# Retention stage: the output projection as three one-pass products on split operands, the decay sums as two

## The reference, cut to what matters

```python
qkvg = x @ w_attn                                  # x normalised; 16 q heads, 8 k and v heads of 64, 8 gates
log_g = jax.nn.log_sigmoid(6.906768 + gates)
q, k = rope(q), rope(k)
log_G = cumsum(log_g, axis=tokens)
s = einsum(q, k) / 8
a = exp(2 * log(|s| + 1e-30) + log_G[t] - log_G[s]), causal, divided by its row maximum
y = (a @ v) / (sum(a) + 1e-6)
y = (y - mean) / sqrt(var + 1e-9) * ln_w           # per head
out = y.reshape(B, T, 1024) @ w_proj
```

## Time and profile before

| | us |
|---|---|
| median of 3 runs | 2173.18 (2172.48 to 2174.24) |
| the profiled execution, its own time | 2173.47 |
| its span, first to last instruction | 2171.4 |
| TensorE busy in it | 2118.3 (98%) |
| VectorE busy | 1390.9 (64%) |
| ScalarE busy | 1397.5 (64%) |
| mean granted TensorE clock | 0.995 of full speed |

### The profile page before, as it was taken

How to read it: one execution, slowest core, us unless ns; L and a number is a source line. 1 busy time by engine, 2 the same in 40 slices (tenths; PEclk the granted TensorE clock), 3 DMA queues, 4 the chain that set the end, 5 groups by cost and what they waited for, 6 DMA issues and landing times. The chain is left out here.

```text
span 2171.4 us, 38655 instructions
## 1 busy us (share of the span) xinstructions
PE 2118.3 (98%) x15079; PEld 1648.6 (76%) x15079; DVE 1390.9 (64%) x2371; ACT 1397.5 (64%) x2701; POOL 308.6 (14%) x277
## 2 busy tenths in 40 slices
PE   8999999999999999899999999999999999998998
PEld 6787778777875667788888857777787787767786
DVE  6455455555565763699999974554545555587897
ACT  3666566666655544788888845666666666556884
POOL 1211112112110000200000211221221221102101
PEclk9999999999999999999999999999999999999999
DMA  4001001010014002799999930101001010013995
GB/s 165 20 21 40 21 21 40 21 40 21 21 30 162 7 33 100 309 372 377 358 345 358 363 134 11 40 21 40 21 20 40 21 40 21 21 59 133 348 402 211
DMA packets 53796, 262.10 MB, mean 121 GB/s; under 512 B 9576, under 2 KB 9960, under 8 KB 26992
## 3 DMA queue, kind: packets, MB, share of 16 engines
q1 hardware_dynamic: 47312, 244.42, 30.0%
q0 software_dynamic: 2560, 8.39, 1.1%
q10 hardware_dynamic: 3744, 6.82, 0.8%
HBM read 243.61 MB, written 15.99 MB: 120 GB/s over the span
## 5 line engine op out<-in xcount | busy, mean ns | idle before, releaser
L645 DVE COPY c_pt<-bank 128x512 f32<-128x512 f32 x256 | 177.2, 692 | 560.7 <-PE bank L443 560.6
L863 ACT ACTIVATE c_pr<-wide,c_nmax 128x512 f32<-128x512 f32 x512 | 348.8, 697 | 120.0 <-DVE c_nmax L637 62.1
L443 PE MATMUL bank<-ident,c_pr 128*128 128x128 f32 x2048 | 266.0, 273 | 1.0 <-ACT c_pt L870 0.7
L443 PEld LDWEIGHTS bank<-ident,c_pr 128*128 128x128 f32 x2048 | 238.2, 140 | 37.5 <-DVE c_pt L645 2.1
L841 ACT ACTIVATE c_khi<-bank,c_cols 128x512 fp32r<-128x512 f32 x128 | 87.9, 687 | 252.2 <-PE bank L95 252.2
L870 ACT COPY c_pt<-bank 128x512 f32<-128x512 f32 x256 | 150.4, 587 | 62.0 <-PE bank L443 61.8
L637 DVE CUSTOM_DVE_ANT_0 wide<-wide,land 128x512 f32<-128x512 f32 x256 | 169.2, 724 | 1.9 <-PE wide L427 1.7
L640 DVE TENSOR_REDUCE c_nmax<-wide 128x1 f32<-128x512 f32 x256 | 158.9, 683 | 1.8 <-PE wide L427 1.7
L312 POOL TENSOR_TENSOR c_clo<-land,c_chi 128x512 fp32r<-128x512 f32 x64 | 82.1, 1287 | 509.0 <-ACT c_chi L827 509.0
L459 PEld LDWEIGHTS bank<-c_pt,c_v 128*32 128x32 f32 x4096 | 104.1, 109 | 49.6 <-issue 47.2
L459 PE MATMUL bank<-c_pt,c_v 128*32 128x128 f32 x4096 | 138.4, 276 | 1.5 <-issue 1.4
(11 more groups left out here) (480 smaller groups left out, 5110.0 us busy)
## 6 DMA issues: line engine op xcount, KB each, us to landing
moe_hr<-in_L_ffn_w SPq DMA_DIRECT2D x68, 1024.0 KB, 7.1
land<-in_L_ffn_w SPq DMA_DIRECT2D x34, 1024.0 KB, 7.0
land<-in_ctx SPq DMA_DIRECT2D x31, 1024.0 KB, 4.9
moe_raw<-in_L_ffn_w SPq DMA_DIRECT2D x18, 1024.0 KB, 6.9
moe_raw<-in_L_ffn_we_gate SPq DMA_DIRECT2D x14, 1024.0 KB, 8.6
land<-in_L_ffn_we_up SPq DMA_DIRECT2D x8, 1024.0 KB, 8.0
moe_raw<-in_L_ffn_we_down SPq DMA_DIRECT2D x8, 1024.0 KB, 8.6
moe_raw<-in_L_ffn_we_up SPq DMA_DIRECT2D x7, 1024.0 KB, 7.6
```

Source lines behind the costliest of these rows:

```text
L443: last = pe.transpose(TB[n % 2][:, h * P:(h + 1) * P], pr[:, u % 2, h, n * P:(n + 1) * P], k["ident"][:])
L645: nc.vector.tensor_copy(pt[:, n, :], TB[0][:]).then_inc(pt_dve, 1)
L863: nc.scalar.activation(pr[:, u % 2, h, :], S[h][:], ACT.Exp, bias=nmax[:, b % 2, i, at:at + 1], scale=-1.0 if masked else 1.0, accum_out=d ...
```

## The change

The weights `wp` are split: ScalarE writes `wp * ln_w` rounded to the one-pass format (float32r) into the tile `home_hi`, and VectorE the rest into `home_lo` (`low_weights`, two instructions of 128x2048, in block 0 behind `standardise(0)`). The turned y is split too: ScalarE's copy becomes `yThi`, and VectorE makes `yTlo` (`low_y`, 128x512 each, two a block). The output product becomes high by high, high by low and low by high, 24 one-pass matmuls in place of 8 fp32 ones. `upto` gets a one-pass copy, made once. The step of the gates is split into two parts of 8 columns, and `cut` becomes two tiles, `cut_hi` and `cut_lo`, each made by one VectorE instruction of 128x1024. The decay sums become 4 one-pass matmuls in place of 2 fp32 ones. ScalarE's copy of y also waits for the product before it.

```diff
-        cut = m.sb("cut", [P, KVH, P])
+        cut_hi, cut_lo = m.sb("cut_hi", [P, KVH, P], F32R), m.sb("cut_lo", [P, KVH, P], F32R)
+        upto_r, step_hi, step_lo = m.sb("upto_r", [P, P], F32R), m.sb("step_hi", [P, KVH], F32R), m.sb("step_lo", [P, KVH])
-        yT = m.sb("yT", [P, 2 * C, P])
+        yThi, yTlo = m.sb("yThi", [P, 2 * C, P], F32R), m.sb("yTlo", [P, 2 * C, P], F32R)
+        wphi, wplo = (tile[:].rearrange("p i (c d) -> p (i c) d", d=D) for tile in k["home"])
...
                 def turn_qk(b):
-                    after(pe, S["y_copied"], 2 * (b - 1))
+                    after(pe, S["y_low"], 2 * (b - 1))
...
                 def sum_decay(b):
-                    pe.wait_ge(S["cut"], b + 1)
-                    pe.wait_ge(S["filled"], 4)
+                    pe.wait_ge(S["upto_r"], 1)
                     after(pe, S["res"], b - 1)
-                    for i in range(2):
-                        pe.matmul(ps[6 + i][:], upto[:], cut[:, i * 4:(i + 1) * 4, :].rearrange("p h s -> p (h s)"),
-                                  start=True, stop=True).then_inc(S["decay_made"], 1)
+                    for n, part in enumerate((cut_hi, cut_lo)):
+                        pe.wait_ge(S["cut"], 2 * b + n + 1)
+                        for i in range(2):
+                            last = pe.matmul(ps[6 + i][:], upto_r[:], part[:, i * 4:(i + 1) * 4, :].rearrange("p h s -> p (h s)"),
+                                             start=(n == 0), stop=(n == 1))
+                            if n == 1:
+                                last.then_inc(S["decay_made"], 1)
...
-                    def multiply(i):
-                        pe.wait_ge(S["wp_done"], 2 * C)
+                    def multiply_high(i):
+                        pe.wait_ge(S["wp_low"], 2)
                         pe.wait_ge(S["y_copied"], 2 * b + i + 1)
                         for c in range(4 * i, 4 * i + 4):
-                            last = pe.matmul(YB[b][:], yT[:, c, :], wp[:, c, :], start=(c == 0), stop=(c == 2 * C - 1))
+                            pe.matmul(YB[b][:], yThi[:, c, :], wphi[:, c, :], start=(c == 0), stop=False)
+                            pe.matmul(YB[b][:], yThi[:, c, :], wplo[:, c, :], start=False, stop=False)
+
+                    def multiply_low(i):
+                        pe.wait_ge(S["y_low"], 2 * b + i + 1)
+                        for c in range(4 * i, 4 * i + 4):
+                            last = pe.matmul(YB[b][:], yTlo[:, c, :], wphi[:, c, :], start=False, stop=(c == 2 * C - 1))
                         return last
...
-                    multiply(0)
+                    multiply_high(0)
                     if b == NB - 1:
+                        multiply_low(0)
                         turn_y(1)
-                    multiply(1).then_inc(S["out_made"], 1)
+                    multiply_high(1)
+                    if b < NB - 1:
+                        multiply_low(0)
+                    multiply_low(1).then_inc(S["out_made"], 1)
...
-                        nc.scalar.activation(wp[:, c, :], wp[:, c, :], ACT.Identity, scale=lnw[:, 0:1]).then_inc(S["wp_done"], 1)
+                        nc.scalar.activation(wphi[:, c, :], wp[:, c, :], ACT.Identity, scale=lnw[:, 0:1]).then_inc(S["wp_done"], 1)
...
+                    after(act, S["out_made"], b)
-                    nc.scalar.copy(yT[:, i * 4:(i + 1) * 4, :].rearrange("p c t -> p (c t)"), ps[4 + i][:]).then_inc(S["y_copied"], 1)
+                    nc.scalar.copy(yThi[:, i * 4:(i + 1) * 4, :].rearrange("p c t -> p (c t)"), ps[4 + i][:]).then_inc(S["y_copied"], 1)
...
+                def cut_parts(b):
+                    s.then(nc.vector.tensor_copy(step_hi[:], gate[:, 5, :]))
+                    s.then(nc.vector.tensor_tensor(step_lo[:], gate[:, 5, :], f32(step_hi[:]), ALU.subtract))
+                    for to, step in ((cut_hi, f32(step_hi[:])), (cut_lo, step_lo[:])):
+                        nc.vector.tensor_tensor(to[:], later[:].unsqueeze(1).to_broadcast([P, KVH, P]),
+                                                step.unsqueeze(2).to_broadcast([P, KVH, P]), ALU.mult).then_inc(S["cut"], 1)
+
+                def low_weights(half):
+                    rows = slice(half * C, (half + 1) * C)
+                    dve.wait_ge(S["wp_done"], (half + 1) * C)
+                    nc.vector.scalar_tensor_tensor(out=wplo[:, rows, :], in0=wp[:, rows, :], scalar=lnw[:, 0:1], in1=f32(wphi[:, rows, :]),
+                                                   op0=ALU.mult, op1=ALU.subtract).then_inc(S["wp_low"], 1)
+
+                def low_y(b, i):
+                    dve.wait_ge(S["y_copied"], 2 * b + i + 1)
+                    after(dve, S["out_made"], b)
+                    nc.vector.tensor_tensor(yTlo[:, i * 4:(i + 1) * 4, :].rearrange("p c t -> p (c t)"), ps[4 + i][:],
+                                            f32(yThi[:, i * 4:(i + 1) * 4, :]).rearrange("p c t -> p (c t)"), ALU.subtract).then_inc(S["y_low"], 1)
...
                     dve.wait_ge(S["filled"], 4)
+                    nc.vector.tensor_copy(upto_r[:], upto[:]).then_inc(S["upto_r"], 1)
+                    cut_parts(0)
...
                     after(dve, S["decay_made"], 2 * b)
+                    cut_parts(b)
...
                     weigh(b)
                     if b + 1 < NB:
                         rotate(b + 1)
+                    if 0 < b < NB - 1:
+                        for i in range(2):
+                            low_y(b - 1, i)
                     if b + 1 < NB:
                         standardise(b, 0, QH)
+                        if b == 0:
+                            low_weights(0)
+                            low_weights(1)
                         if b > 0:
                             add_output(b - 1)
                         if b + 2 < NB:
                             scale(b, 0, QH)
                 scale(NB - 2, 0, QH)
                 for i in range(2):
+                    low_y(NB - 2, i)
+                for i in range(2):
                     standardise(NB - 1, i * KVH, KVH)
                     scale(NB - 1, i * KVH, KVH)
+                low_y(NB - 1, 0)
                 add_output(NB - 2)
                 dve.wait_ge(S["res"], NB - 1)
                 for b in range(NB - 1):
                     measure_rows(nc, s, k, x, b)
+                    if b == 0:
+                        low_y(NB - 1, 1)
                 add_output(NB - 1)
```

More of the change, by code:

```diff
@@ L995, in stage_retention @@
                   "scores", "abs", "r_ready", "squared", "a_turned", "a_copied", "num", "num_read", "yvar", "ystd", "y_ready",
-                  "y_turned", "y_copied", "lnw_in", "wp_done", "sums", "final", "out_made", "res", "stored"):
+                  "y_turned", "y_copied", "y_low", "lnw_in", "wp_done", "wp_low", "upto_r", "sums", "final", "out_made", "res", "stored"):
             S[n] = m.sem(n)
@@ L1340, in cut_decay @@
                     dve.wait_ge(S["filled"], 4)
-                    nc.vector.tensor_tensor(cut[:], later[:].unsqueeze(1).to_broadcast([P, KVH, P]),
-                                            gate[:, 5, :].unsqueeze(2).to_broadcast([P, KVH, P]), ALU.mult).then_inc(S["cut"], 1)
+                    nc.vector.tensor_copy(upto_r[:], upto[:]).then_inc(S["upto_r"], 1)
+                    cut_parts(0)
                 def rotate_first():
```

## The result

The changed kernel takes 2190.97 us (median of 5, 2190.83 to 2194.9) against 2173.18 before (2172.48 to 2174.24): 1.0087 times, 95% interval 1.0076 to 1.0097, so 17.8 us slower. The forecast was 2175.4, at most 2179.0. The profiled execution took 2190.83, with a span of 2188.9; the one before 2173.47 and 2171.4.

The account below looks back on a forecast made before the run. TensorE was busy 98% of the span, with VectorE close behind where they meet. Terms +0.75 + 1.25 + 0.3 + 0.3 - 0.4 = +2.2 us gave 2175.7 against the profiled execution, 2175.4 against the median; range 2172.8 to 2179.0.

Parts of the forecast that it names:

- the clock rival: New TensorE pauses let the clock fall: one fall gives 2176.9 us, two 2178.4; chance 0.28, of it 0.15 two or more.
- Steps 1 and 2: Blocks 0 and 1: VectorE's split work puts block 1's scores at +0.75 us; `low_weights` then bring block 1's end to +2.0.
- the rival of hidden additions: VectorE's additions delay nothing, so all 9.6 us of TensorE's saving shows: 2163.6 us; chance 0.05.
- Step 3: Blocks 2 and 3: TensorE waits 2.7 us for VectorE's addition ahead of the decay sums; net +0.3 us per block.
- Step 4: The stage's end, block 3: the last products end some 0.4 us earlier than the shift from earlier steps says.
- The pause of 2.2: Block 3, at the end: TensorE idles 2.2 us ahead of `multiply_low(0)`, waiting for `low_y(3, 0)` on VectorE.
- The sum without the clock: All steps of the stage together, with no added clock falls: +2.2 us.
- Cheap `low_weights`: `low_weights` run at no cost to `weigh(1)`, so step 2's 1.25 us falls away: +0.95 us, 2174.1; chance 0.08.
- a fifth dearer: VectorE's new instructions take a fifth more than their rows: +4.5 us in all, 2177.7; chance 0.04.

Follow-up runs that it names:

- the filled kernel: The changed kernel plus TensorE products that nothing reads in its pauses, VectorE's work unchanged: 2178.11 us against 2173.53 before, ratio 1.0019.
- the added pause: The kernel before plus four VectorE instructions nobody reads (3.9 us) ahead of `standardise` in blocks 1 and 2: 2187.89 us, ratio 1.0064.

## Why the prediction was wrong

**The step that failed is the price and the chance of the clock rival.** The forecast let the clock be, since one pause in the earlier trace rows had full speed behind it and one half speed. It priced a fall at 1.5 us, from one stretch of 3 us, and left 0.15 to two falls or more. The trace of before has two more pauses of over 2 us in its later stages, and both have half speed behind them; here they are, with a window behind each:

```profile
910.15 0.65 PE L93 MATMUL bank<-moe_whi,moe_hhi 128*128 128x512 f32 x1 [2.45 <-DVE moe_hlo L2293]
...
2021.19 0.76 PE L93 MATMUL wide<-moe_whi,moe_xThi 128*128 128x512 f32 x1 [3.33 <-DVE moe_xTlo L2238]
...
910.20:913.20 3.00, 3.00 (x8) 2.33 (x9) 3.00 (x2) 3.00 (x6) 0.00 (x0) 0.51 0.99 418
2021.20:2026.20 5.00, 5.00 (x12) 3.94 (x13) 4.24 (x2) 0.40 (x1) 0.00 (x0) 0.50 0.92 345
```

So three such pauses of four had a fall, and one of the falls lasted some 7 us, from inside its pause on. In the profiled execution all four new pauses are followed by half speed, and a fifth fall comes in the next stage. The stretches are about 6.8, 10.2, 10.2, 3.4 and 3.4 us. At half speed a stretch costs about half its length less what was waited or idle there: the last addition of the changed kernel is at 833.74 and that of the filled one at 821.76, 12.0 us; with 1.6 in the next stage that is 13.6. The medians, which hold the falls of all other stages too, differ by 12.9. So a fall cost from 1.6 us to about 5. The rival had two of the places and the kind of consequence right, but half the price (13.6 / 5 = 2.7 on the mean) and far too small a count, and the range ended below it. The mistake in reasoning was to read two rows that disagree as a reason for a middling chance of one fall; they were two draws, and the change added four more. With even odds for each of four pauses, two falls or more would have had 11 chances in 16, and by the trace's three of four still more.

The prediction cites the Trainium skill, "TensorE: Matmul & The Clock Gate", section "HAM oscillation — how this bites in real kernels", for the array going back to its slow state at each pause between bursts. The page says it of a kernel whose waits last some 3 to 5 us; three of the four new pauses are shorter. The four bear it out all the same; over all runs it holds often and not always (below).

**Steps 1 and 2 held.** scores(1): forecast 714.57, measured 714.67. The transposes of block 1: forecast 733.85; with the clock kept up, 733.87 (736.00 in the changed kernel, the fall ahead of them). `low_weights` 4.61 (4.4), `low_y` 1.28 (1.27), second `cut` tile 744.04 - 742.90 = 1.14 (1.14). One-pass products are 743.25 to 747.06 for 16, 0.238 each with the slower start of the first, against 0.227; the 0.217 worked out in the rival of hidden additions is further off.

**Step 3 held but for 0.2 us a block.** Its wait came out: from the last gate to the decay sums it is 753.23 - 742.29 = 10.94 us, and 10.95 was forecast. TensorE arrived 1.27 and not 1.5 earlier, so the pauses are 2.31 and 2.29 and not 2.7. What was too good is the price of the sums, 1.11 us and not 0.91. Scores(3) come at +3.1 with the clock kept up, against +2.6.

**Step 4 failed, by 1.05 us.** The end gave +0.65 (3.75 - 3.1) in place of -0.4. It took the first half's turn and copy as one step of 1.4, and so passed over the root of the second half, which stands ahead of that copy on ScalarE; mending that order gave 0.86 of it back. The pause of 2.2 was put ahead of `multiply_low(0)`; it came one step earlier, 3.67 long. Its own fall, 3.4 us long, came on top. With ScalarE's order mended the forecast pause did appear, at 1.80.

**The sum without the clock** was +2.2 and measured +3.75 in the filled kernel's trace, +4.6 in its median, 2178.1. That is within the range, at its upper end. The rival of hidden additions falls: the pauses stand where VectorE ends, and TensorE's saving would have been 7.9 us and not 9.6. Cheap `low_weights` falls too as the change has them, though another place made them so. VectorE's prices were not a fifth dearer.

## What to carry to other kernels

When work moves from TensorE to another engine, list every new wait of TensorE and its length before adding up durations: each of 2 us or more is also a likely fall of the clock (9 of 11 in this stage), and that may cost more than the wait. Where the room on the other engine is 1 or 2 us at each meeting point, the order of its list can matter more than the amount of work, as it did here; do first what someone waits for (here the added output and the copy of y), and put the rest where that engine already waits. If a wait can't be avoided, products that nothing reads kept the clock up in both kernels tried.

## What the runs showed of the hardware that was not expected

**Whether the clock falls differs from execution to execution and kernel to kernel behind the same pause.** The 2.23 us pause ahead of the next stage stands in all thirteen traces; half speed follows it in eight. At the stage's start, with gaps of 1.76 and 0.68 us, it follows in six. Behind pauses of 2.3 to 3.7 us within the stage it followed nine times of eleven; the exceptions are the 2.84 above and the 3.28 ahead of kr. Gaps of up to 1.2 us mostly left it alone, but not always. A fall can begin while TensorE still stands (in the added pause, and ahead of 2021.19 in the kernel before). What decides was not found; the spread of the executions (the kernel before alone: 2170.95 to 2176.2) is of its size.

**The half-speed stretches had several lengths**, about 3.4, 6.8, 10.2 and once 13.6 us, though TensorE had no gap after their first 3 us. Why the fall behind one pause ends after 3 us and behind another after 10 stays open.

**VectorE's instructions took up to 3.5 times as long beside GpSimd** when both read tiles in SBUF (2.38 us and not 0.68), and no longer than alone for reductions out of PSUM (0.42). GpSimd's own 128x1024 product took 2.80 or 2.81 us where VectorE takes 1.22; it always began 0.2 us behind the start of VectorE's `cut_hi`, so no run shows what it takes alone.
